# The chain to the first cross-attention queries, and the order in which a decoder layer starts its first maximum rounds

## The reference

```python
x = x + self_attention(layernorm(x), qkv_w, qkv_b, proj_w, proj_b)   # 56 keys per batch
x = x + cross_attention(layernorm(x), ctx, bias, Wq, Wk, Wv, Wo)     # 1500 keys per batch
x = x + mixture_of_experts(layernorm(x), Wg, W1, W2, W3, Ws1, Ws2, Ws3)
```

## Time and profile before

| | us |
|---|---|
| median of 3 runs | 483.22 |
| lowest and highest | 479.52 and 484.08 |
| profiled execution | 482.8 |
| its span | 481.1 |
| PE, DVE, ACT, POOL busy | 424.2, 350.7, 319.4, 298.3 |

### The profile page before, as it was taken

One profiled execution on the slowest core, in us unless ns is written; L12 is line 12 of the kernel. 1 busy time (PEld: TensorE's weight loads), 2 busy tenths in 40 slices (PEclk: granted clock), 3 DMA queues, 4 the chain that ended last, 5 costly groups with the idle time before them and its releaser, 6 DMA issues.

```text
span 481.1 us, 16300 instructions
## 1 busy us (share of the span) xinstructions
PE 424.2 (88%) x6928; PEld 291.9 (61%) x6928; DVE 350.7 (73%) x544; ACT 319.4 (66%) x675; POOL 298.3 (62%) x249
## 2 busy tenths in 40 slices
PE   3338958788999999999999999999978989889996
PEld 2125746265676676776766776766745665555674
DVE  7364437986877777878777778777786953768796
ACT  6325622376878887887888788788846867464563
POOL 7779476999677586685685685676918271434100
PEclk9999976699999999999999999999989989999999
DMA  6477348646947957857749678665323000000000
GB/s 157 144 133 136 111 94 212 129 148 164 193 148 102 219 126 129 181 156 137 177 131 168 163 123 125 113 135 151 123 64 83 4 3 1 1 0 1 25 1 18
DMA packets 78120, 53.30 MB, mean 111 GB/s; under 512 B 62968, under 2 KB 69216, under 8 KB 78048
## 3 DMA queue, kind: packets, MB, share of 16 engines
q1 hardware_dynamic: 76136, 50.88, 47.8%
q0 software_dynamic: 1248, 0.85, 0.7%
q10 hardware_dynamic: 664, 0.52, 0.3%
HBM read 17.05 MB, written 0.46 MB: 36 GB/s over the span
## 4 chain that ended last, share of the span: by engine, by line
PE 71%; DVE 12%; ACT 5%; POOL 5%; issue 3%; DMA 2%; ACTq 1%; SPq 1%; DVEq 0%; POOLq 0%
PE ps L1026 18%; PE ps L860 12%; PE ps L1002 7%; PE ps L373 4%; PE ps L375 4%; PE ps L374 4%; DVE mx L1620 3%; PE ps L863 3%; PE ps L1156 3%; PE ps L788 2%; PE ps L791 2%; PE ps L789 2%; PE ps L870 2%; DVE mself L1486 2%; PE ps L893 2%
## 5 line engine op out<-in xcount | busy, mean ns | idle before, releaser
L1620 DVE TENSOR_REDUCE mx<-ps 120x2 f32<-120x1000 f32 x192 | 221.2, 1195 | 61.6 <-PE ps L1002 61.6
L1320 ACT ACTIVATE p<-ps 125x448 f32<-125x448 f32 x288 | 141.7, 549 | 19.8 <-PE ps L1026 16.3
L1026 PE MATMUL ps<-qall,ks 128*125 128x224 f16 x768 | 128.9, 274 | 4.6 <-DMA qall<-mrow 1.7
L1026 PEld LDWEIGHTS ps<-qall,ks 128*125 128x125 f16 x768 | 77.3, 138 | 42.8 <-issue 19.7
L619 POOL TENSOR_TENSOR k<-k,zero 128x500 f16<-128x500 f32 x48 | 48.8, 1018 | 66.3 <-ACT k L1246 53.6
L860 PE MATMUL ps<-p,v 125*27 125x168 f32 x1152 | 65.4, 313 | 0.1
L623 POOL TENSOR_TENSOR k<-k 128x500 f16<-128x500 f32 x48 | 55.3, 1152 | 3.8
L1320 ACT ACTIVATE wnat<-ps 125x448 f32<-125x448 f32 x96 | 47.1, 541 | 9.1 <-PE ps L1026 8.9
L605 POOL TENSOR_TENSOR ch<-ctx,ch 128x1536 f16<-128x1536 f32 x16 | 49.7, 3109 | 1.5 <-DMA ct<-ch 0.3
L1002 PE MATMUL ps<-ks,qall 31*56 31x500 f16 x768 | 43.5, 406 | 4.8 <-DVE mx L1620 3.1
L595 POOL TENSOR_TENSOR ch<-ctx,zero 128x1536 f16<-128x1536 f32 x16 | 43.9, 2747 | 2.4 <-issue 2.3
(11 more groups left out here) (198 smaller groups left out, 773.5 us busy)
## 6 DMA issues: line engine op xcount, KB each, us to landing
ks<-k SPq DMA_DIRECT2D x48, 375.0 KB
ctx<-in_ctx SPq DMA_DIRECT2D x16, 672.0 KB
ctx<-in_L_ffn_W SPq DMA_DIRECT2D x48, 64.0 KB, 2.1
ks<-brow SPq DMA_DIRECT2D x32, 46.9 KB
ctx<-in_ctx SPq DMA_DIRECT2D x16, 78.0 KB
ct<-ch SPq DMA_TRANSPOSE x32, 6.3
qall<-q POOLq DMA_DIRECT2D x12, 42.0 KB, 3.2
xs<-in_x SPq DMA_DIRECT2D x1, 448.0 KB, 3.9
```

The costliest lines, as they stand in the source:

```text
L1026: last = mm(stb[score_bank(r, c, s, half)][0:KP, 224 * (g % 2):224 * (g % 2) + 224], ks[c % 3][:, g, KP * s:KP * s + KP], qall[:, g, :, 3 ...
L1320: A(p[s % 4][0:KP, 448 * half:448 * half + 448], stb[score_bank(r, c, s, half)][0:KP, 0:448], ACT.Exp, scale=SCALE).then_inc(exp_done, 1)
L1620: V.tensor_reduce(mx[:, h:h + 2, k // 2], mxb[0:120, 2 * pair:2 * pair + 2, 0:CH], axis=AX.X, op=ALU.max).then_inc(mx_read, 1)
```

## The change

Four edits, none of which adds or removes arithmetic. (1) Inside the self steps the links of the first chain move ahead: the output projection of step 5 before that step's product and pick, DVE's addition and statistics and `norm_apply` before its `normalize`, the transposes and `norm_out` from step 7 to the end of step 6, the projection and q1 at step 7 ahead of the key projection. (2) Self steps 9 and 10 and `value_project(0, 0, 0)` now stand before round 0, and the output projection of tiles 2 to 6 with DVE's addition and statistics right behind round 0, not behind round 2. (3) ACT issues no query DMA: SP issues six and POOL six. (4) On POOL `rstd_of(1, 1)` stands before `split_keys(1, j)`, and POOL waits for `nbias` before `split_first(3)`.

```diff
-        qx_ok = [[sem("qx0_sp"), sem("qx0_pool"), sem("qx0_act")], [sem("qx1_pool")]]
+        qx_ok = [[sem("qx0_sp"), sem("qx0_pool")], [sem("qx1_pool")]]
...
             query_rows(sp, 1, 0, 0, 0, qx_ok[0][0])
+            sp.wait_ge(q2_ok, 3)
+            query_rows(sp, 1, 0, 2, 1, qx_ok[0][0], (0, 1))
             load_ctx(3)
...
-            query_rows(pool, 1, 0, 2, 1, qx_ok[0][1], (0,))
+            query_rows(pool, 1, 0, 2, 1, qx_ok[0][1], (2, 3))
             split_first(2)
             split_second(2)
+            rstd_of(1, 1)
             for j in range(3):
                 split_keys(1, j)
-            rstd_of(1, 1)
+            pool.wait_ge(nbias_ok, 1)
             split_first(3)
...
-                if s == Q_STEP:
-                    pe.wait_ge(chain_read, 1)
-                    transpose_norm(1, 0, 3, chain_psum)
...
-                if s == OUT_STEP:
-                    pe.wait_ge(misc_read, self_index(s, "tr") + 1)
-                    out_project(0, 0, chain_bank, chain_psum)
...
+                if s == Q_STEP - 1:
+                    pe.wait_ge(chain_read, 1)
+                    transpose_norm(1, 0, 3, chain_psum)
 
             pe.wait_ge(pick_ok, 1)
-            for s in range(PAIRS + 1):
+            for s in range(PAIRS + 3):
                 self_step(s)
...
+            value_project(0, 0, 0)
             max_round(0, -2, 2, 0)
-            self_step(PAIRS + 1)
-            value_project(0, 0, 0)
+            pe.wait_ge(misc_read, BEFORE_LOOP)
+            out_project(0, 1, flat_bank(0, 640), o_psum)
             max_round(0, -2, 2, 1)
-            self_step(PAIRS + 2)
             value_project(0, 0, 1)
             max_round(0, -2, 2, 2)
-            pe.wait_ge(misc_read, BEFORE_LOOP)
-            out_project(0, 1, flat_bank(0, 640), o_psum)
             value_project(0, 0, 2)
...
             take_round(0, -2, 2, 0)
-            self_step(PAIRS + 1)
-            take_round(0, -2, 2, 1)
-            take_round(0, -2, 2, 2)
             dve.wait_ge(o_psum, 1)
             add_to_x(LN_TILES[1][1], flat_bank(0, 640), x_ok)
             dve.wait_ge(x_ok, 1)
             norm_stats(1, 1)
+            take_round(0, -2, 2, 1)
+            take_round(0, -2, 2, 2)
             iteration(0, -1)
```

More of the change, by code:

```diff
@@ L927, in self_step @@
                     tr(turn_bank(s)[:, 0:128], tok[:], ident[:]).then_inc(misc_done, 1)
+                if s == Q_STEP:
+                    pe.wait_ge(xt2_ok, 3)
+                    a, z = QX[0]
+                    split_matmul(chain_bank[:, 0:z - a], wt1[:, CROSS_W], wt2[:, CROSS_W], xt1[:, a:z], xt2[:, a:z]
+                                 ).then_inc(chain_psum, 1)
                 if s in PREP:
@@ L930, in self_step @@
                     prepare[use[0]](0, b, int(use[1]))
+                if s == OUT_STEP:
+                    pe.wait_ge(misc_read, self_index(s, "tr") + 1)
+                    out_project(0, 0, chain_bank, chain_psum)
                 if 0 <= s - 1 < PAIRS:
@@ L992, in max_round @@
                     else:
-                        for n, sent in enumerate((4, 5, 3)):
-                            pe.wait_ge(qx_ok[0][n], sent * 16)
+                        for sent in qx_ok[0]:
+                            pe.wait_ge(sent, 6 * 16)
                     pe.wait_ge(*keys_in(r, c + off))
@@ L1275, in self_step @@
                       scale=SCALE).then_inc(exp_done, 1)
-                if s == Q_STEP:
-                    norm_out(1, 0, 3, chain_psum, 2)
                 if 0 <= s - 3 < PAIRS:
@@ L1280, in self_step @@
                     A(attn[:, 2 * S * (s - 3):2 * S * (s - 2)], turn_bank(s)[:, 0:2 * S], ACT.Copy).then_inc(misc_read, 1)
+                if s == Q_STEP:
+                    act.wait_ge(chain_psum, 3)
+                    a, z = QX[0]
+                    A(q1[:, a:z], chain_bank[:, 0:z - a], ACT.Copy).then_inc(q1_ok, 1)
                 if s in PREP:
@@ L1289, in self_step @@
                       ps[:, 6:8, 0:224].rearrange("p u (k q) -> p u k q", k=4), ACT.Copy).then_inc(o_read, 1)
-                if s == Q_STEP:
-                    act.wait_ge(chain_psum, 3)
-                    a, z = QX[0]
-                    A(q1[:, a:z], chain_bank[:, 0:z - a], ACT.Copy).then_inc(q1_ok, 1)
-                    act.wait_ge(q2_ok, 3)
-                    query_rows(act, 1, 0, 2, 1, qx_ok[0][2], (1, 2, 3))
+                if s == Q_STEP - 1:
+                    norm_out(1, 0, 3, chain_psum, 2)
             self_max_rows(0)
             self_max_rows(1)
-            for s in range(PAIRS + 2):
+            for s in range(PAIRS + 3):
                 self_step(s)
-            take_values(0, 0, 0)
-            self_step(PAIRS + 2)
-            for j in (1, 2):
+            for j in range(3):
                 take_values(0, 0, j)
@@ L1541, in self_step @@
                     V.tensor_tensor(q2[:, a:z], chain_bank[:, 0:z - a], q1[:, a:z], ALU.subtract).then_inc(q2_ok, 1)
+                if s == 0:
+                    dve.wait_ge(bias_step, 2)
+                    V.scalar_tensor_tensor(bias_lo, bias_lo, -BIG, braw_rows[32:48], ALU.mult, ALU.add).then_inc(brow_ok, 1)
+                if 0 <= s - 2 < PAIRS:
+                    dve.wait_ge(misc_done, self_index(s, "sel") + 1)
+                    normalize(s - 2, pick_bank(s), 2 * S, rec_pair, misc_read)
+                if s == 2:
+                    V.tensor_tensor(xs[:], xs[:], bp[:].rearrange("p (o d) -> p o d", o=1).to_broadcast([128, TT, D]),
+                                    ALU.add).then_inc(xb_ok, 1)
+                if s == Q_STEP - 1:
+                    norm_out(1, 0, 3, xt2_ok)
             dve.wait_ge(ones_ok, 1)
-            for s in range(PAIRS + 1):
+            for s in range(PAIRS + 2):
                 self_step(s)
```

16 lines of the change are left out of this document (removed).

## The result

The change makes the kernel slower by a little under 1%: 485.48 us (median of 20 executions, 482.83 to 489.25) against 482.05 (20 executions, 479.52 to 486.76), a ratio of 1.0081 with a 95% interval of 1.0060 to 1.0103. In a second session it was 486.27 against 482.68, ratio 1.0095 (1.0061 to 1.0128). The forecast was 480.9. Every ratio here leaves out executions more than 1.5% above the fastest of their kernel; in the whole study that is one, of 489.00 us, of the kernel with edit 4 undone.

The account below looks back on a forecast made before the run. The bound was when POOL can begin its twelve query DMAs (98.35), on which iteration 1's start hangs. Starting them at 96.4 gains 1.95 us: 482.8 - 1.95 = 480.85, say 480.9 us; range 478.3 to 484.0.

Parts of the forecast that it names:

- q1 of the first tiles: First chain moved ahead: q1 at 60.8 instead of 62.86, a gain of 2.0 us.
- `nbias` without a neighbour on POOL: DVE's nbias, no longer held by POOL's context split, takes 0.2 us instead of 1.51 and ends at 83.4.
- rival B: On DVE, nbias keeps its 1.51 us for its own reason, ending at 84.7; 0.65 gained, 482.2 us; chance 0.08.
- POOL deciding: POOL's list, not q1 of tiles 2 to 6 (95.5), sets the twelve query DMAs at 96.4; 1.95 us gained.
- self steps 9 and 10 and values ahead of round 0: PE before round 0: pairs at 2.2 us each plus 0.7 of values, so round 0 at 68.7, 69.9 at half clock.
- now the gaps are under 1 us each: PE in the self steps: short idle gaps instead of 63.6 to 65.9, so 68.7 is taken for round 0.
- point of decision: Rival C decides where nbias ends later than 98.35 - 12.95 = 85.4; 12.95 is POOL's work from nbias to the twelve DMAs.
- rival C: POOL starves behind its nbias wait: clock falls in self steps, twelve DMAs at 98.7; 0.35 lost, 483.2 us; chance 0.17.
- The maxima's DMA: POOL issues batch 0's maxima at 93.7; in flight 3.2 us, landing at 96.9, where scores start (before 98.64).
- The gain is kept to the end: In the loop, PE fills each iteration from iteration 1, so its 1.95 us earlier start lasts to the end.
- Iteration 0's work on PE took 18.4: Carried over from before: PE ready at 115.3, ahead of POOL's chain at 116.8, so the wait before iteration 1 stays.
- this edit uses up what the DMAs gave: Self steps and values ahead of round 0 leave it only 0.3 us before the old 69.03.

## Why the prediction was wrong, by its own steps

**What held.** q1 of the first tiles (60.8 forecast, 60.84 measured). SP's six issues (the sixth near 65; six took 4.91 us from 60.91). `nbias` without a neighbour on POOL (0.2 forecast, 0.15; 1.17 and 1.90 where the split ran beside it), which rules out rival B. POOL idle 1.6 us before the context split (1.80). POOL deciding, no wait before the twelve DMAs. The loop's 18.66 us from one iteration to the next is the same in every profile up to the eleventh. (The prediction's 19.72 us were the length of a window, not of an iteration: in the kernel before iteration 1 starts at 118.78 and iteration 2 at 137.44. The sum doesn't use it.)

**The step that failed first** is "self steps 9 and 10 and values ahead of round 0": 68.7 was taken "if the clock stays up", with 69.9 as the other end. The clock fell (pick of 1.71 us at 66.46), and 70.59 lies beyond even that end: pairs of self steps and values together cost 1.9 more than forecast. The low clock is 1.5 of it: 0.74 in the last pick and 0.7 in the values, which took 1.42 (69.17 to 70.59) and not 0.7. The rest is the pick of pair 5, which ended 0.2 late, and the pairs, which took 2.5 and 2.4 us from pick to pick where the working has 2.2. The argument "now the gaps are under 1 us each" was true (0.74 and 0.35) and did not help.

**The sizes that followed.** The statistics ended at 76.2 (forecast 74.0), round 3 ended at 85.7 (forecast 83.2), `nbias` at 85.76 (83.4). The forecast's own point of decision was 85.4, and it was passed. POOL's list then ran as computed: 98.85 instead of 96.4. This is rival C, forecast for 98.7 and with a chance of 0.17. "It decides where `nbias` ends later than 85.4" was right, and in hindsight the chance was small: the rows of before already had PE at half clock from 69.03 on, and the edit put more waiting work in front of that.

**The steps that were mis-sized, C included.** (a) The maxima's DMA: forecast in flight for 3.2 us for batch 0, measured 3.4 to 3.9 in the four profiles, with the scores at 100.11 instead of 96.9 behind up to 3.33 us of idle PE. For batch 1 the forecast kept the landing of before; it was 3.61 then, and 3.87 and 4.37 in two executions with the same issue time. Iteration 1 started on that landing in all four profiles, at 118.67 to 120.04 where 116.8 was forecast. Sending both from ACT gave the whole loss back. (b) "The gain is kept to the end" took everything behind iteration 1 as a constant. Up to the eleventh iteration it is one, but the late part took 52.16 to 54.33 us in kernels that have the same work there. (c) "Iteration 0's work on PE took 18.4" was carried over as well. It was 17.8 to 20.2 in the four profiles, but PE was ready before the DMA each time, so this decided nothing here.

With what the start loses in the four profiles (-0.1 to +1.3 us) the sum would be 482.7 to 484.1, around rival C's 483.2. The median of 485.48 lies above that, and what adds the remainder in most executions isn't shown.

**The part whose gain was real** is the first one. Alone it gives 1.5 us, because round 0 then starts 1.3 us early and everything after it moves. The forecast took "this edit uses up what the DMAs gave" for the combination, and that was right in kind: with the other edits, above all the self steps and values put in front of round 0, that round starts 2.8 us later (70.59 against 67.75).

## What to carry to other kernels

Moving a chain's links ahead pays only until something else is put in the place it freed: edit 1 gave 1.5 us, and the reordering that came with it took 4.9. Before an in-order engine is made to wait for a value, list every transfer queued behind the wait and ask who waits for each; here a list that ran late held two DMAs of 1.8 KB on which the next iterations hung, and issuing them from the engine that makes the data undid the loss. A profile that is the fastest of its executions understates a loss, so take one near the median too, and where even that shows less than the medians, say so.

## What the runs showed of the hardware

- A small DMA issued by POOL (1.8 KB, batch 0's maxima) landed 1.6 to 3.9 us after its issue. It took 1.6 in the kernel with edit 4 undone, where the DMA engines' share from 94 to 98 us was 0.00; 2.7 and 2.5 in the kernel before, at 0.35; and 3.4 to 3.9 in four profiles of the changed one, at 0.86 to 0.98, with SP's context loads in flight. The same DMA for batch 1 took 3.0 to 5.1 us. A higher share went with a longer landing from kernel to kernel; no run varied it alone, so it isn't shown to be the reason.
- The DVE operation with two SBUF inputs over 5 elements a partition took 0.15 us with POOL waiting, and 1.17, 1.51 and 1.90 where a POOL split ran beside it, ending within 0.03 us of the split each time. The rule in the Trainium skill, "SBUF — State Buffer", section "Who interferes with whom", on the port pair that the two share agrees. Removing the collision by a wait moved its cost to POOL: without the wait the changed kernel took 484.04 us, with it 485.48 and 486.27.
- A late stretch of the loop took 25.3 to 25.7 us in the profiles with a granted clock of 0.94 from 350 to 380 us, and 26.95 to 27.2 in those with 0.83, in kernels with the same instructions there. The difference is over a third of the measured loss. One profile at 0.89 took 28.05, so the mean over that window doesn't give the time by itself.
